# A graph attention, linear attention and expert layer: a middle stage with four fewer GpSimd operations and another order on every engine

## The reference, cut to what matters

```python
xn = layernorm(x)                                   # x: 12500 x 256
x = x + gnn(xn, src, dst) + mix(xn)                 # src, dst: 200000
x = x + ffn(layernorm(x))
# gnn: xt = xn @ weight, per token i (only the first 12500 edges count):
#   alpha = softmax_h(leaky_relu(l[src[i]] + r[dst[i]])); sum_h alpha_h * xt[dst[i], h]
# mix: q = elu(xn Wq)+1, k = elu(xn Wk)+1; per head q (k^T v) / max(q . sum k, 1e-6); times Wproj, plus bproj
# ffn: expert = argmax(logits), prob = max softmax; position by a running count per expert, capacity 1563;
#   relu(x w1 + b1) w2 + b2, times prob, back at the token's place
```

## Time and profile before

| | |
|---|---|
| median of three runs | 1539.72 us (1539.47 to 1540.53) |
| the profiled execution, its own time | 1540.95 us |
| its span, first to last instruction | 1539.1 us |
| busy over the span | PE 1426.4 (93%), PEld 1282.6 (83%), DVE 1122.5 (73%), ACT 952.0 (62%), POOL 727.3 (47%) |
| q1 (SyncE's DMA queue) | 72.73 MB, 19.0% of 16 engines |
| q0 (GpSimd's DMA queue) | 38.82 MB, 11.5% |
| mean granted TensorE clock | 0.943 of 2.4 GHz |

### The profile page before, as it was taken

One profiled execution on the slowest core, in us unless ns is written; L12 is line 12 of the kernel. 1 busy time (PEld: TensorE's weight loads), 2 busy tenths in 40 slices (PEclk: granted clock), 3 DMA queues, 4 the chain that ended last, 5 costly groups with the idle time before them and its releaser, 6 DMA issues. The chain is left out here.

```text
span 1539.1 us, 30428 instructions
## 1 busy us (share of the span) xinstructions
PE 1426.4 (93%) x9008; PEld 1282.6 (83%) x9008; DVE 1122.5 (73%) x2832; ACT 952.0 (62%) x2017; POOL 727.3 (47%) x704
## 2 busy tenths in 40 slices
PE   5999999998799898899579999999999999999995
PEld 4999999997677777777469999999999999999994
DVE  5888888883678778778536867767776776877764
ACT  2555555542477777777556767667676676767662
POOL 1100000003788888888243446445446445455533
PEclk8999999997788988988779999999999999999998
DMA  4434333333344444445312121213113131122000
GB/s 85 87 80 80 86 83 74 86 73 74 93 111 109 117 109 111 116 109 157 73 31 78 31 57 44 71 39 97 43 40 91 40 95 43 39 69 53 7 15 19
DMA packets 128116, 112.13 MB, mean 73 GB/s; under 512 B 66078, under 2 KB 113887, under 8 KB 127946
## 3 DMA queue, kind: packets, MB, share of 16 engines
q1 hardware_dynamic: 75206, 72.73, 19.0%
q0 software_dynamic: 52864, 38.82, 11.5%
HBM read 76.17 MB, written 43.85 MB: 78 GB/s over the span
## 5 line engine op out<-in xcount | busy, mean ns | idle before, releaser
L1390 POOL DMA_INDIRECT out<-q_all,to_i x128 | 176.3, 1378 | 328.6 <-issue 293.8
L1592 DVE TENSOR_TENSOR h_lo<-q_all,h_hi 128x496 fp32r<-128x496 f32 x256 | 173.8, 679 | 197.7 <-PE psY L1653 88.4
L1468 ACT ACTIVATE h_hi<-psH,b_sb 128x496 fp32r<-128x496 f32 x256 | 172.6, 674 | 232.7 <-PE psH L1676 225.7
L1653 PE MATMUL psY<-w_hi,h_hi 128*124 128x256 f32 x1024 | 289.2, 282 | 0.0
L1653 PE MATMUL psY<-w_hi,h_lo 128*124 128x256 f32 x1024 | 287.1, 280 | 0.0
L1653 PE MATMUL psY<-w_lo,h_hi 128*124 128x256 f32 x1024 | 286.8, 280 | 0.0
L1653 PEld LDWEIGHTS psY<-w_lo,h_hi 128*124 128x124 f32 x1024 | 188.9, 184 | 8.9
L1653 PEld LDWEIGHTS psY<-w_hi,h_hi 128*124 128x124 f32 x1024 | 188.8, 184 | 8.0
L1377 POOL DMA_INDIRECT q_all<-out,from_i x112 | 164.5, 1469 | 54.8 <-issue 54.8
L1653 PEld LDWEIGHTS psY<-w_hi,h_lo 128*124 128x124 f32 x1024 | 189.1, 185 | 0.0
L1470 ACT ACTIVATE q_all<-psH,b_sb 128x496 f32<-128x496 f32 x256 | 170.8, 667 | 0.0
(11 more groups left out here) (241 smaller groups left out, 3366.6 us busy)
## 6 DMA issues: line engine op xcount, KB each, us to landing
x_sb<-in_x SPq DMA_DIRECT2D x50, 448.0 KB
q_all<-in_L_ffn_w SPq DMA_DIRECT2D x16, 1024.0 KB
graph_table<-tab_sb SPq DMA_DIRECT2D x25, 511.0 KB
out<-xd SPq DMA_DIRECT2D x25, 448.0 KB
x_sb<-in_x SPq DMA_DIRECT2D x50, 52.0 KB
out<-q_all,to_i POOLq DMA_INDIRECT x128, 4.3
q_all<-out,from_i POOLq DMA_INDIRECT x112, 4.5
gl<-alpha_l_table,idx POOLq DMA_INDIRECT x100
```

Of the source, the lines that this page charges most:

```text
L1390: pool.indirect_dma_start(out=out, in_=o_sb[:, par, j, :], in_offset=None, out_offset=bass.IndirectOffsetOnAxis(ap=to_i[:, par, j:j + 1], ...
L1468: act.activation(h_hi[:, f % 4, :], psH[f % 2][:, 0:TS3], ACT.Relu, bias=b1_sb[:, bass.ds(e * NF + f, 1)]).then_inc(s_hhi_ready, 1)
L1592: nc.vector.tensor_tensor(h_lo[:, f % 4, :], hf[:, f % 4, :], h_hi[:, f % 4, :].bitcast(F32), ALU.subtract).then_inc(s_hlo_ready, 1)
L1653: ins = nc.tensor.matmul(psY[par][j // 2][0:T3, (j % 2) * D:(j % 2 + 1) * D], hh[:, f % 4, j * T3:(j + 1) * T3], w[:, f, :], start=f == 0 ...
```

## The change

In the middle stage, and two constants of the first:

- Token numbers for all steps are made once by two iotas (tok_all, ntok_all); `token_of` is gone. The index copies become SyncE DMAs from SBUF to SBUF. The xl copy of the steps moves to ScalarE. GpSimd's step is the eight gathers.
- Denominators go one step further ahead: q_ksum(s+3), inverse(s+2), den_of(s+2), inverse_t(s+2), den_spread(s+2), q_copy(s+4), with three of them moved ahead of the steps at the start. In ScalarE's program att_exp(0) stands behind inverse_t(1) and q_copy(3).
- VectorE runs q_scaled right behind den_of, ahead of logits. place has another order.
- ScalarE makes one-hots for j = 0 to 2 in one_hots(s), for j = 3 after root(s+1); TensorE's listed is cut likewise, with q_ksum and inverse between.
- den_spread comes after mix; mix goes over feature halves outside, over j inside.
- The loop covers two steps less.

```diff
@@ -121,8 +121,8 @@
-tokn = sb("tokn", [T, J])
-ntokn = sb("ntokn", [T, J])
+tok_all = sb("tok_all", [T, NS * J])
+ntok_all = sb("ntok_all", [T, NS * J])
@@ -322,9 +322,9 @@
-        nc.gpsimd.iota(tokn[:, :], [[1, J]], base=1 - TS, channel_multiplier=J,
+        nc.gpsimd.iota(tok_all[:, :], [[TS, NS], [1, J]], base=1, channel_multiplier=J,
...
-        nc.gpsimd.iota(ntokn[:, :], [[-1, J]], base=TS - 1, channel_multiplier=-J,
+        nc.gpsimd.iota(ntok_all[:, :], [[-TS, NS], [-1, J]], base=-1, channel_multiplier=-J,
@@ -723,26 +724,25 @@
-    s_token = sem_in(ph, "s_token")
...
+    idx_in = [s_idx0, s_idx1]
...
-        step(0, 0, 0, 2)
-        step(1, 1, 0, 2)
-        with eng.Fori(1, (NS - 3) // 2) as i:
-            step(2 * i, 0, i, 2)
-            step(2 * i + 1, 1, i, 2)
-        step(NS - 3, 0, (NS - 3) // 2, 2)
-        step(NS - 2, 1, (NS - 3) // 2, 1)
-        step(NS - 1, 0, NS // 2, 0)
+        step(0, 0, 0, 4)
+        step(1, 1, 0, 4)
+        with eng.Fori(1, (NS - 5) // 2) as i:
+            step(2 * i, 0, i, 4)
+            step(2 * i + 1, 1, i, 4)
+        for s in range(NS - 5, NS):
+            step(s, s % 2, s // 2, NS - 1 - s)
@@ -765,16 +765,27 @@
+        def idx_of(s, par, n):
...
+            sp.wait_ge(gat[par], 32 * J * n)
+            sp.dma_start(idx[:, par, :, :], idx_all[:, bass.ds(s, 1), :, :].rearrange("p a n j -> p (a n) j"))\
+              .then_inc(idx_in[par], 16)
...
+        for s in range(2):
+            sp.dma_start(idx[:, s, :, :], idx_all[:, s, :, :]).then_inc(idx_in[s], 16)
...
+        idx_of(2, 0, 1)
...
-            if ahead == 2:
+            if ahead > 1:
...
-            if ahead == 2 and isinstance(s, int) and s == NS - 3:
+                if not (isinstance(s, int) and s + 3 >= NS):
+                    idx_of(s + 3, 1 - par, h + par + 1)
+            if ahead > 1 and isinstance(s, int) and s == NS - 3:
@@ -783,14 +794,8 @@
     def _(pool):
-        def idx_of(s, par, n):
...
-            pool.wait_ge(gat[par], 32 * J * n)
-            nc.gpsimd.tensor_copy(idx[:, par, :, :], idx_all[:, bass.ds(s, 1), :, :].rearrange("p a n j -> p (a n) j"))\
-              .then_inc(s_idx, 1)
...
-        def gather(s, par):
-            pool.wait_ge(s_idx, s + 1)
+        def gather(s, par, n):
+            pool.wait_ge(idx_in[par], 16 * n)
             passed(pool, s_pool_passed)
@@ -798,34 +803,16 @@
-        def xl_of(s, par):
-            pool.wait_ge(s_mix_mm, 2 * (s - 1))
-            nc.gpsimd.tensor_copy(x_sb[0:T, par, :, D:MW],
-                                  xl_all[:, bass.ds(s, 1), :, :].rearrange("p a j e -> p (a j) e")).then_inc(s_xl, 1)
...
-        def token_of(s):
-            pool.wait_ge(s_at_ready, 3 * J * s)
-            passed(pool, s_pool_passed)
-            nc.gpsimd.tensor_scalar(tokn[:, :], tokn[:, :], float(TS), None, ALU.add).then_inc(s_token, 1)
-            nc.gpsimd.tensor_scalar(ntokn[:, :], ntokn[:, :], float(TS), None, ALU.subtract).then_inc(s_token, 1)
...
-        idx_of(0, 0, 0)
-        idx_of(1, 1, 0)
-        gather(0, 0)
-        gather(1, 1)
-        idx_of(2, 0, 1)
+        gather(0, 0, 1)
+        gather(1, 1, 1)
         pool.wait_ge(s_bg_done, 2)
...
         def step(s, par, h, ahead):
-            if ahead == 2:
+            if ahead > 1:
                 pool.wait_ge(s_pr, NPR * s + 1)
-                gather(s + 2, par)
-                if not (isinstance(s, int) and s + 3 >= NS):
-                    idx_of(s + 3, 1 - par, h + par + 1)
-                xl_of(s + 2, par)
-            token_of(s)
+                gather(s + 2, par, h + 2)
@@ -845,6 +832,15 @@
+        def hots(s, j):
+            act.activation(at_row[:, j, :], away[:, j, 0:T3], ACT.Relu, bias=1.0, scale=-1.0)\
+               .then_inc(s_at_ready, 1)
+            act.activation(at_block[:, j, 0, :], away[:, j, T3:T3 + NB], ACT.Relu,
+                           bias=tok_all[:, bass.ds(s * J + j, 1)], scale=ntok_all[:, bass.ds(s * J + j, 1)])\
+               .then_inc(s_at_ready, 1)
+            act.activation(at_block[:, j, 1, :], away[:, j, T3:T3 + NB], ACT.Relu, bias=prb[:, j:j + 1],
+                           scale=nprb[:, j:j + 1]).then_inc(s_at_ready, 1)
@@ -853,6 +849,12 @@
+        def xl_of(s, par):
+            act.wait_ge(s_mix_mm, 2 * (s - 1))
+            act.activation(x_sb[0:T, par, :, D:MW],
+                           xl_all[:, bass.ds(s, 1), :, :].rearrange("p a j e -> p (a j) e"), ACT.Copy)\
+               .then_inc(s_xl, 1)
@@ -881,14 +883,9 @@
-            act.wait_ge(s_token, 2 * (s + 1))
...
-            for j in range(J):
-                act.activation(at_row[:, j, :], away[:, j, 0:T3], ACT.Relu, bias=1.0, scale=-1.0)\
-                   .then_inc(s_at_ready, 1)
-                for n, (v, nv) in enumerate(((tokn, ntokn), (prb, nprb))):
-                    act.activation(at_block[:, j, n, :], away[:, j, T3:T3 + NB], ACT.Relu, bias=v[:, j:j + 1],
-                                   scale=nv[:, j:j + 1]).then_inc(s_at_ready, 1)
+            for j in range(J - 1):
+                hots(s, j)
@@ -904,17 +901,25 @@
             root(s)
-            if ahead > 0:
-                inverse_t(s + 1)
+            if not (isinstance(s, int) and s == 0):
+                hots(s - 1, J - 1)
             if ahead > 1:
-                q_copy(s + 2)
+                inverse_t(s + 2)
             logit_exp(s)
...
                 att_exp(s + 1)
+            if ahead > 3:
+                q_copy(s + 4)
+            if ahead > 1:
+                xl_of(s + 2, par)
+            if ahead > 0:
                 one_hots(s)
...
+        q_copy(2)
+        inverse_t(1)
+        q_copy(3)
         att_exp(0)
@@ -939,9 +944,9 @@
+            dve.wait_ge(s_inv_mm, s)
...
-            dve.wait_ge(s_inv_mm, s)
@@ -1033,34 +1038,35 @@
-            dve.wait_ge(s_l_exp, s + 1)
-            nc.vector.tensor_reduce(lsum[:, :], lex[:, :, :], axis=AX.X, op=ALU.add).then_inc(s_route, 1)
             dve.wait_ge(s_pos_mm, s + 1)
...
             dve.wait_ge(s_route, NROUTE * s + 8)
+            nc.vector.tensor_reduce(slotf[:, :], picked[:, :, :], axis=AX.X, op=ALU.add).then_inc(s_route, 1)
+            dve.wait_ge(s_route, NROUTE * s + 10)
             dve.wait_ge(s_at_ready, 3 * J * s)
-            nc.vector.reciprocal(prb[:, :], lsum[:, :]).then_inc(s_place, 1)
-            dve.wait_ge(s_route, NROUTE * s + 9)
-            nc.vector.tensor_reduce(slotf[:, :], picked[:, :, :], axis=AX.X, op=ALU.add).then_inc(s_route, 1)
-            dve.wait_ge(s_route, NROUTE * s + 11)
             nc.vector.tensor_scalar(blk[:, :], slotf[:, :], 1.0 / T3, 0.5 / T3 - 0.5, ALU.mult, ALU.add)\
               .then_inc(s_place, 1)
+            dve.wait_ge(s_l_exp, s + 1)
+            nc.vector.tensor_reduce(lsum[:, :], lex[:, :, :], axis=AX.X, op=ALU.add).then_inc(s_route, 1)
+            dve.wait_ge(s_place, NPLACE * s + 1)
+            nc.vector.tensor_scalar(blk[:, :], blk[:, :], ROUND, ROUND, ALU.add, ALU.subtract).then_inc(s_place, 1)
+            dve.wait_ge(s_route, NROUTE * s + 11)
+            nc.vector.reciprocal(prb[:, :], lsum[:, :]).then_inc(s_place, 1)
             dve.wait_ge(s_place, NPLACE * s + 2)
-            nc.vector.tensor_scalar(blk[:, :], blk[:, :], ROUND, ROUND, ALU.add, ALU.subtract).then_inc(s_place, 1)
-            dve.wait_ge(s_place, NPLACE * s + 3)
             nc.vector.scalar_tensor_tensor(row[:, :], blk[:, :], -float(T3), slotf[:, :], ALU.mult, ALU.add)\
...
             rows_of(s, par, h)
+            if ahead > 1:
+                den_of(s + 2)
             if ahead > 0:
-                den_of(s + 1)
+                q_scaled(s + 1)
             logits(s)
...
                 att_scores(s + 1, 1 - par, h + par + 1)
-                q_scaled(s + 1)
             place(s)
@@ -1076,15 +1082,15 @@
+        den_of(1)
...
-        dve.wait_ge(s_token, 2 * NS)
...
-            for n, v in enumerate((tokn, prb)):
-                nc.vector.tensor_scalar(at_block[:, j, n, :], upto[:, T3:T3 + NB], blk[:, j:j + 1], v[:, j:j + 1],
+            for n, v in enumerate((tok_all[:, (NS - 1) * J + j:(NS - 1) * J + j + 1], prb[:, j:j + 1])):
+                nc.vector.tensor_scalar(at_block[:, j, n, :], upto[:, T3:T3 + NB], blk[:, j:j + 1], v,
@@ -1104,14 +1110,14 @@
-        def q_ksum(s):
+        def q_ksum(s, copied):
...
-            pe.wait_ge(s_inv_t, s)
+            pe.wait_ge(s_inv_t, copied)
...
-            if not (isinstance(s, int) and s < 2):
-                pe.wait_ge(s_route, NROUTE * (s - 2) + 9)
+            if not (isinstance(s, int) and s < 4):
+                pe.wait_ge(s_route, NROUTE * (s - 4) + 8)
@@ -1125,7 +1131,7 @@
-        q_ksum(0)
+        q_ksum(0, 0)
@@ -1169,19 +1175,19 @@
-            pe.wait_ge(s_qp_done, KC * (s + 1))
-            for j in range(J):
-                for kc in range(KC):
+            for kc in range(KC):
+                pe.wait_ge(s_qp_done, KC * s + kc + 1)
+                for j in range(J):
```

(41 more changed lines are left out.)

## The result

The changed kernel takes 1525.68 us (median of four runs, 1523.24 to 1529.61), the kernel before 1540.12 beside it: ratio 0.9909, interval 0.9887 to 0.9931. So it is 14.4 us faster, where 29.6 were forecast, and 1.7 us above the range. The profiled execution took 1526.20, its span is 1524.5.

What follows compares the result with a forecast made beforehand. GpSimd, full at 14.4 us a step, was taken as the bound. First lg at 410.1 + 24 steps x 12.75 + 3.5 = 719.6, not 748.19; with the end -29.6 us, so a median of 1510 us, range 1497 to 1524.

Steps and rivals of the forecast that it cites:

- What bounds the kernel now: Middle stage: GpSimd is full at 14.4 us a step; ScalarE's one-hots wait for it, so the next root starts late.
- GpSimd: Middle stage: 2.5 us of copies and token operations go; eight gathers and 0.1 of waiting leave 12.3 a step.
- rival of late indices (d): Middle stage: the index DMA comes 1 to 2 us late each step; 14.0 a step, 1539 us, no change; chance 0.03.
- VectorE's cycle: Middle stage: VectorE's own work takes 12.1 us a step (11.9 to 12.4), with 0.2 taken off for place's new order.
- ScalarE: Middle stage: 11.1 us of work a step with the xl copy; att_exp at 7.3, before VectorE asks at 7.8.
- rival (e): Middle stage: ScalarE becomes the bound at 13.6 us a step, 1530 us; by the drain 13.9, about 1536; chance 0.04.
- TensorE: Middle stage: 11.6 us of matmuls plus 1.1 lost at half clock, 12.7 a step, with hardly any wait.
- two thirds: Middle stage, TensorE: share kept of the 1.7 us a step lost at half clock, taken as 1.1 (0 to 1.7).
- Rival (b): Middle stage: TensorE is the bound at today's clock, 11.6 / 0.88 = 13.2 us a step, 1520 us; chance 0.21.
- Rival (a): Middle stage: TensorE's clock stays at 2.4 GHz, the step is GpSimd's 12.3 us, 1499 us in all; chance 0.18.
- Start: Middle stage's start: att_exp(0) comes at 405.6 and the first lg at 410.1, not 401.88; 8.2 us lost.
- End: Middle stage's end: last gather beside expert weights, wait 3.8 us, +3.5 on the 24 steps; last root earlier, -1.0.

Runs made afterwards that it cites:

- the wide filler: Changed kernel with q_ksum in halves between listed's matmuls and one needless 256-column matmul behind den_spread: 1509.22 us, 0.9795 of the kernel before.
- the thin filler: Against the kernel with the wide filler: two needless matmuls of 8 columns in place of the 256-column one; 1526.98 us, 0.9922 of the kernel before.
- place put back: Against the kernel with the wide filler: VectorE's place alone in the old order, lsum ahead of picked; 1533.77 us, 0.9953 of the kernel before.
- the best version: Kernel with the wide filler plus att_exp(0) first, expert weights behind the last gather, two first xl copies on ScalarE: 1489.38 us, 0.9665; run again, 1487.97.

## Why the prediction was wrong, point by point

**What bounds the kernel now** was right. GpSimd held the step: lightening it alone gave 12.3 of the 14.4 us. That TensorE would be the next bound was right too.

**GpSimd**, forecast 12.3 (bound 12.2 and 0.1 of waiting): right. No wait for an index DMA, and 12.44 where it is the bound (the wide filler). The rival of late indices (d) fell.

**VectorE's cycle**, 12.1 (11.9 to 12.4): right for the use made of it. Short steady steps took 12.2, in the changed kernel and with the filler; the same instructions took 11.66 at 704.4, where hardly anything was waited for. One term was mis-sized: place, 0.2 us a step, is worth 24.6 / 24 = 1.0 with interleaving and filler. My own numbers held part of it. I let the second of the two exponents, att_exp, come at 7.3 and compared that with att_sum at 7.8; but the first one, at 7.1, is lsum's, and lsum, in the old order, would have asked at 2.5 + 1.26 + 2.1 + 0.8 = 6.7, with all of place behind it. That is 0.4 us; 0.8 were measured at full clock, and most of the rest of the loss is the low clock that comes back with the wait. As the new order was part of the change, the sum didn't suffer; the reason given for it did. The mix by halves was priced at nothing, and is worth nothing that could be told.

**ScalarE**: no drain behind the table load, which still takes 1.28, with the exponent 10 ns behind it (569.23, 570.52); nothing waits for the root. So rival (e) fell, and with it the bound of 13.9 that the drain of the Trainium skill, ScalarE: Activation LUTs, section What ACT_TABLE_LOAD costs, would give. ScalarE waits 2.2 us a step at inverse_t, one half of a sign that I had set for being wrong; the other half, VectorE waiting in att_sum, didn't come.

**TensorE** is the step that failed: "11.6 + 1.1 = 12.7, and hardly any wait", and from it the step of **12.75**. Measured were 13.16, and 22 x 0.41 = 9.0 us is the largest part of the miss. Over the 22 steps from 427.76 to 716.48 TensorE took 288.72 / 22 = 13.12 a step, which divide into 11.8 of work at full clock, 1.1 of low clock and 0.2 of waiting. So the work was 0.2 too small (the mix takes 3.74, not 3.6, and den_spread 1.98, not 1.9), and the waiting 0.2 where I had put nearly nothing.

The loss to the clock was, on average, what I had put, but by luck: "two thirds" had no reason behind it, and no step loses two thirds. Fourteen of the 22 mixes lose 5.42 - 3.74 = 1.7, the whole of it (one of them 1.5), and eight lose nothing: 25.0 us with one slow stretch more, 1.1 a step. The forecast added the mean to the work, as if each step paid it. But a step that pays takes 13.48, and one that doesn't can't fall to 11.8: it meets the 12.2 to 12.4 of the other engines, and TensorE waits there for lg. That is the 0.2. I left "what steps of unlike length lose" at 0.05.

Rival (b) has the step, 13.2, but by another sum: 11.6 at the old clock of 0.88. The clock rose to 0.91; 11.8 / 0.91 is 13.0, and the waiting makes up the rest.

Rival (a), full clock because the idle time goes, fell: the wait ahead of the mix went, and the mix was still slow in 14 steps, in eleven of them with no idle time since the mix before. The rule that it was cited with (the Trainium skill, TensorE: Matmul & The Clock Gate, A second HAM failure mode: psum-queue depth-cycling) puts a swinging clock down to short idle times. In these runs idle time isn't needed for the low clock: with the thin filler nine of ten slow x_parts had no gap ahead, and stood behind thin work; a wide filler in its place ended it. Nor is it enough: behind 0.55 us of it at 545.77 x_part takes 2.05. But it isn't without effect either, as the kernel with place put back shows (0.96 with the wide filler and idle time, 1.00 without).

**Start**: the first lg at 411.1 for 410.1, att_exp(0) at 406.4 for 405.6, by the chain that I had worked out. What I left out is the step behind it: TensorE had idled for 4.05 us and then ran x_part and q_ksum at half clock (0.57 over the step), so it took 15.38, 2.6 more than the 12.75 put for it. That the idle time is the cause isn't shown: with the first exponent moved ahead it was gone, and the step took 16.14.

**End**: the wait was 6.68 us, not 3.8. I had the mechanism (the transfers don't get faster while the step does; with the weights behind the gather the wait is gone) but sized it by one step's gain of 1.7. Why the two now collide more isn't traced. The step took 17.91, not 12.75 + 3.5 = 16.25: 1.7 more. Behind the last lg stand 1526.20 - 733.95 = 792.25 us, where it was 1540.95 - 748.19 = 792.76: a gain of 0.5, not 1.0.

The sum: 1.0 (start) + 2.6 (first step) + 9.0 (22 steps) + 1.7 (last step) + 0.5 = 14.8 us over the forecast, of 1526.20 - 1511.3 = 14.9. The chances put 0.21 on (b), but its own time, 1520, took the first step and the end from the forecast. The range ended at 1524, (b) with a dearer end; the dearer end came, and the slow first step, in no rival, on top of it.

What stays open: why some steps of one program keep the full clock and others don't, with the same instructions in the same order; how much of the low clock is owed to thin work and how much to idle time where both are there; what the unnamed wait on the slower chip is; and how much of the first step (19 us in the best version) could still go.

## What to carry to other kernels

When an engine is relieved, ask which one takes the bound, and at which clock: TensorE at 98% busy still ran at half clock behind thin matmuls. If a loss falls whole on some steps and not at all on others, don't add its mean to the work. Price the two kinds of step apart, the fast kind by the next bound, and average then: here 14 steps of 13.5 and 8 of about 12.3 give 13.05, where adding the mean loss of 1.1 to a work of 11.8 gives 12.9.

Spread thin matmuls between wide ones, and try one needless wide matmul behind a thin stretch; measure it, since without the right place it costs what it brings. When an instruction is moved ahead of another on an engine that runs in the order of the text, ask for every reader of what now comes later when it asks, not only the one you have in mind: the place order, nearly worthless on paper, was worth 1.6%.

## What the runs showed of the hardware

- With the same share of busy time on TensorE (257.4 and 257.6 of 260 us), fillers of 8 columns left the granted clock at 0.94 and one of 256 columns gave 1.00; the kernel went from 0.9922 to 0.9795.
- With the same wide filler but idle time of mostly 0.5 to 1.1 us before x_part (place put back, 244.7 of 260 us busy) the clock was 0.96.
- The half clock isn't tied to one operation. It fell on the mix, and with the thin work split, on x_part (2.04 became up to 3.73).
- One gain at the start (first lg 8.1 us earlier) was lost within the stage, most of it to the clock (0.90 to 0.87 over 430 to 690 us): without a steady clock, a part's worth can't be read from its place.
- The kernel before took 1539.6 to 1540.9 us (medians) on four chips and 1591.7 on a fifth; comparisons hold only beside a kernel that ran on the same one.
